# Edge matrix of a graph layer on one Trainium2 core: bank opening by one flag, matmuls in three rounds, 120 key columns

## The reference

```python
h = layernorm(x); acc = h
for _ in range(3):
    h = segment_sum(edge_weight[:, None] * h[dst], src)     # rows of h gathered and summed by node
    h = h / max(norm(h), 1e-12)
    acc = acc + h
x = x + acc / 4
x = x + layernorm(y + moe(y)) * gamma + beta                # y = layernorm(x)
```

## Time and profile before

| | us |
|---|---|
| median of 3 runs (1508.99 to 1516.28) | 1509.21 |
| the profiled execution | 1510.28 |
| its span in the trace | 1508.6 |
| TensorE matmuls busy | 1294.8 |
| DVE busy | 1113.5 |
| ACT busy | 883.1 |
| POOL busy | 248.7 |

### The profile page before, as it was taken

One profiled execution on the slowest core, in us unless ns is written; L12 is line 12 of the kernel. 1 busy time (PEld: TensorE's weight loads), 2 busy tenths in 40 slices (PEclk: granted clock), 3 DMA queues, 4 the chain that ended last, 5 costly groups with the idle time before them and its releaser, 6 DMA issues. The chain is left out here.

```text
span 1508.6 us, 31442 instructions
## 1 busy us (share of the span) xinstructions
PE 1294.8 (86%) x9378; PEld 1110.7 (74%) x9379; DVE 1113.5 (74%) x1946; ACT 883.1 (59%) x1937; POOL 248.7 (16%) x233
## 2 busy tenths in 40 slices
PE   4588888888799999999999999999977799999800
PEld 1466666767588888888888888888853799999800
DVE  8888989999676656766655766655567688998768
ACT  1678888888755555655555655555341566666522
POOL 1400000000040000000000000000031578887600
PEclk8799999999999999999999999999986899999955
DMA  5088888888886666656666656666322787334384
GB/s 186 28 207 196 201 199 197 203 202 209 216 233 208 184 184 180 194 170 189 182 189 184 190 164 185 178 189 182 113 91 89 238 272 218 108 105 106 89 289 143
DMA packets 225441, 267.36 MB, mean 177 GB/s; under 512 B 15763, under 2 KB 168066, under 8 KB 225298
## 3 DMA queue, kind: packets, MB, share of 16 engines
q1 hardware_dynamic: 211932, 240.41, 58.0%
q0 software_dynamic: 7680, 20.98, 4.8%
q10 hardware_dynamic: 5760, 5.25, 1.4%
HBM read 175.51 MB, written 91.07 MB: 177 GB/s over the span
## 5 line engine op out<-in xcount | busy, mean ns | idle before, releaser
L844 PE MATMUL ps_rows<-h_both,a_high 128*128 (+1 forms) x1875 | 506.2, 398 | 10.5 <-ACT halves L592 5.3
L684 DVE TENSOR_TENSOR a_low<-a_raw,a_high 128x640 fp32r<-128x640 f32 x375 | 305.6, 823 | 233.7 <-ACT a_high L578 230.4
L578 ACT ACTIVATE a_high<-a_raw 128x640 fp32r<-128x640 f32 x375 | 274.6, 740 | 287.6 <-PE ps_rows L847 265.6
L844 PEld LDWEIGHTS ps_rows<-h_both,a_high 128*128 128x128 f32 x1875 | 330.2, 191 | 68.6 <-ACT halves L592 14.4
L847 PEld LDWEIGHTS ps_rows<-h_both,a_low 128*128 128x128 f32 x1875 | 276.1, 191 | 32.9
L847 PE MATMUL ps_rows<-h_both,a_low 128*128 (+1 forms) x1875 | 284.9, 283 | 0.0
L821 PEld LDWEIGHTS ps_w<-lo_hot,key_w 128*128 128x128 bf16 x2736 | 196.1, 98 | 85.2 <-issue 83.9
L821 PE MATMUL ps_w<-lo_hot,key_w 128*128 128x160 bf16 x2736 | 211.4, 234 | 48.1 <-issue 38.0
L560 ACT ACTIVATE win<-ps_w 128x480 f32<-128x480 f32 x304 | 148.8, 575 | 56.3 <-PE ps_w L826 32.6
L668 DVE TENSOR_TENSOR key_w<-key_hot,tab_marks 128x1536 bf16<-128x1536 bf16 (+1 forms) x228 | 173.8, 817 | 0.0
L551 ACT ACTIVATE key_w<-key_hot,third_b 128x128 bf16<-128x128 bf16 x456 | 144.8, 428 | 5.6 <-DVE key_hot L659 3.1
(11 more groups left out here) (233 smaller groups left out, 1627.4 us busy)
## 6 DMA issues: line engine op xcount, KB each, us to landing
a_raw<-a_rows SPq DMA_DIRECT2D x375, 320.0 KB, 3.2
a_rows<-win SPq DMA_DIRECT2D x228, 240.0 KB, 3.6
w_raw<-in_L_ffn_w SPq DMA_DIRECT2D x32, 512.0 KB
a_rows<-win SPq DMA_DIRECT2D x76, 180.0 KB
b_t<-in_L_ffn_b ACTq DMA_DIRECT2D x40, 128.0 KB, 3.4
hf<-in_x SPq DMA_DIRECT2D x1, 3072.0 KB
x<-in_x SPq DMA_DIRECT2D x1, 3072.0 KB
tokens<-hf SPq DMA_DIRECT2D x4, 768.0 KB
```

The source lines that it names most:

```text
L578: a.activation(a_high[:, u, :], a_raw[:, u, :], ACT.Copy).then_inc(high_split, 1)
L684: v.tensor_tensor(a_low[:, u, :], a_raw[:, u, :], a_high[:, u, :].bitcast(F32), ALU.subtract).then_inc(low_split, 1)
L844: nc.tensor.matmul(ps[:, banks[w][r], :], a_high[:, u, r * P:(r + 1) * P], both, start=first, stop=False, skip_group_check=True)
```

## The change

It does these things:

- From batch 2 on the four opening matmuls write 16 columns in place of 512. In the first two batches, one for each half of PSUM, they still write 512.
- Columns that no matmul of a batch touches now keep what was there before. Two things follow. The carry must not read a stale window: `fresh` marks batches whose first window isn't shared with the batch before, and their carry reads the zero slot. And a batch's store may write stale rows past its last window, which later stores overwrite, except past the end: so the zeros over those rows are written last (`pad`, after load 14 of the first pass) from the zero slot of `win`, and SP's load of chunk 24 and POOL's constants wait for it. The padding at the start, its memset and its wait go.
- The 36 matmuls of a batch run in three rounds, one for each weight part, over the twelve steps. Each round waits for its own part alone.
- The key one-hots, their weighted copies, the stationary side of the matmuls and the rows of PSUM that they write have 120 columns (`M`) in place of 128.

```diff
@@ phase_tables
-            g.iota(tab.key_tab[:, 0:M, :], pattern=[[1, M], [0, 2]], base=0, channel_multiplier=0, **kw)
-            g.memset(tab.key_tab[:, M:P, :], -2.0)
+            g.iota(tab.key_tab[:], pattern=[[1, M], [0, 2]], base=0, channel_multiplier=0, **kw)
...
+            link(v.memset(fresh[:, 0:1], 0.0))
+            link(v.tensor_tensor(fresh[:, 1:s.NB], base[:, 1:s.NB], by_batch[:, 0:s.NB - 1, B - 1], ALU.subtract))
+            link(v.scalar_tensor_tensor(moved[:], fresh[:], float(B), moved[:], ALU.mult, ALU.add))
@@ phase_layers, sync
-            first = s.W * CW
-            sp.wait_ge(tabs, 3)
-            sp.dma_start(a_dram.rearrange("i (c n) l -> (i c) (n l)", c=CW)[first:s.CH * P, :],
-                         zeros[0:s.CH * P - first, :]).then_inc(padded, 16)
...
-            sp.wait_ge(padded, 16)
+            def pad():
+                for done in stored:
+                    sp.wait_ge(done, 16 * NB)
+                sp.dma_start(a_dram[s.W:s.W + PADDING, :, :].rearrange("i p l -> p i l"),
+                             win[0:M, 0, B * LO:(B + 1) * LO].unsqueeze(1).broadcast_to(
+                                 [M, PADDING, LO])).then_inc(padded, 16)
...
+                if j == CH - 1:
+                    sp.wait_ge(padded, 16)
                 load(0, j)
                 if j in LAST:
                     store(LAST[j], LAST[j] % WINS)
+                if j == PAD_AT:
+                    pad()
@@ gpsimd
             g.memset(none[:], 0.0).then_inc(tabs, 1)
-            g.memset(zeros[:], 0.0).then_inc(tabs, 1)
...
-            for done in stored:
-                pool.wait_ge(done, 16 * NB)
+            pool.wait_ge(padded, 16)
@@ vector
-                v.tensor_tensor(key_w[:, u, k, 0:n, :, :], key_hot[:, u, 0:n, :, :], mark(b, 2 + k, P)[:, 0:n, :, :],
+                v.tensor_tensor(key_w[:, u, k, 0:n, :, :], key_hot[:, u, 0:n, :, :], mark(b, 2 + k, M)[:, 0:n, :, :],
@@ tensor
+                wide = 16 if late(b, 2) else 512
                 for bank in range(BANKS):
-                    mm(ps_w[:, u, bank * 512:(bank + 1) * 512], none[:, 0:P], none[:, :],
+                    mm(ps_w[:, u, bank * 512:bank * 512 + wide], none[:, 0:P], none[:, 0:wide],
                        start=True, stop=False, skip_group_check=True)
...
-                pe.wait_ge(hot_ready, (b + 1) * 4)
-                pe.wait_ge(third_ready, (b + 1) * BY_ACT)
-                for j in range(B):
-                    for k in range(3):
-                        ins = mm(ps_w[:, u, bass.DynSlice(places[j], LO)], key_w[:, u, k, j // 2, :, j % 2],
+                for k in range(3):
+                    pe.wait_ge(hot_ready, b * 4 + (2 + k))
+                    if k == 2:
+                        pe.wait_ge(third_ready, (b + 1) * BY_ACT)
+                    for j in range(B):
+                        ins = mm(ps_w[0:M, u, bass.DynSlice(places[j], LO)], key_w[:, u, k, j // 2, :, j % 2],
                                  lo_hot[:, u, j // 2, :, j % 2],
                                  start=False, stop=False, skip_group_check=True)
```

More of the change, by code:

```diff
@@ L128, in phase_tables @@
         moved = sb("moved", [1, s.NB])
+        fresh = sb("fresh", [1, s.NB])
         fields = sb("fields", [1, s.NB, 2 * s.ROW])
@@ L378, in phase_layers @@
         LAST = {6: NB - 2, 10: NB - 1}
+        PAD_AT = 14
+        PADDING = -(-(CH * P) // CW) - s.W
         a_raw = sb("a_raw", [P, RING, G * P])
@@ L407, in phase_layers @@
             lo_hot, key_hot, key_w = [early.enter_context(nc.sbuf_tensor(name, shape, BF16)) for name, shape in (
-                ("lo_hot", [P, 2, PAIRS, LO, 2]), ("key_hot", [P, 2, PAIRS, P, 2]), ("key_w", [P, 2, 3, PAIRS, P, 2]))]
+                ("lo_hot", [P, 2, PAIRS, LO, 2]), ("key_hot", [P, 2, PAIRS, M, 2]), ("key_w", [P, 2, 3, PAIRS, M, 2]))]
             ps_w = early.enter_context(nc.psum_tensor("ps_w", [P, 2, BANKS * 512], F32))
@@ L411, in phase_layers @@
         ps = ctx.enter_context(nc.psum_tensor("ps_rows", [P, NBANK, 2 * D], F32))
-        zeros = a_raw[:].rearrange("p u c -> p (u c)")
         block = ctx.enter_context(nc.Block())
@@ L509, in _ @@
             g.memset(none[:], 0.0).then_inc(tabs, 1)
-            g.memset(zeros[:], 0.0).then_inc(tabs, 1)
             g.memset(win[:, :, B * LO:(B + 1) * LO], 0.0).then_inc(tabs, 1)
             g.memset(ones[:], 1.0).then_inc(tabs, 1)
-            pool.wait_ge(tabs, 4)
+            pool.wait_ge(tabs, 3)
             g.affine_select(out=ident[:], in_=ones[:], pattern=[[1, P]], compare_op=ALU.is_equal,
@@ L658, in one_hots @@
                     dve.wait_ge(third_ready, (b - 1) * BY_ACT)
-                v.tensor_tensor(key_hot[:, u, :, :, :], tab.key_tab[:].unsqueeze(1).broadcast_to([P, PAIRS, P, 2]),
-                                mark(b, 0, P), ALU.is_equal).then_inc(key_ready, 1)
+                v.tensor_tensor(key_hot[:, u, :, :, :], tab.key_tab[:].unsqueeze(1).broadcast_to([P, PAIRS, M, 2]),
+                                mark(b, 0, M), ALU.is_equal).then_inc(key_ready, 1)
                 v.tensor_tensor(lo_hot[:, u, :, :, :], tab.lo_tab[:].unsqueeze(1).broadcast_to([P, PAIRS, LO, 2]),
@@ L794, in _ @@
             mm = nc.tensor.matmul
-            pe.wait_ge(tabs, 5)
+            pe.wait_ge(tabs, 4)
             def multiply(b, i):
@@ L825, in multiply @@
                     pe.wait_ge(windows_out, b)
-                    ins = mm(ps_w[:, u, bass.DynSlice(places[0], LO)], ident[:, :],
+                    ins = mm(ps_w[0:M, u, bass.DynSlice(places[0], LO)], ident[:, 0:M],
                              win[:, (i - 1) % WINS, bass.DynSlice(slot, LO)],
@@ L1696, in __init__ @@
         self.lo_tab = sb("lo_tab", [P, s.LO, 2], BF16)
-        self.key_tab = sb("key_tab", [P, P, 2], BF16)
+        self.key_tab = sb("key_tab", [P, s.M, 2], BF16)
         self.marks = sb("tab_marks", [P, 5, s.STEPS], BF16)
```

## The result

| | before | after |
|---|---|---|
| median, us | 1511.90 (4 runs, 1508.99 to 1516.28) | 1561.47 (4 runs, 1560.03 to 1566.89) |
| ratio to before, 95% interval | | 1.0334 [1.0303, 1.0365] |
| the profiled execution | 1510.28 | 1562.75 |
| its span | 1508.6 | 1560.9 |

The change makes the kernel 3.3% slower; the forecast was 1570. It rested on +60.8 us, and +52.5 was measured between the profiled executions. From the page of the kernel after: the busy times, the TensorE clock granted in each fortieth of the span and the DMA share.

The account below looks back on a forecast made before the run. TensorE's sequencer was taken to bound the edge-matrix stage: 74 batches at 5.54 us give +62.7, the end -1.9, so +60.8 on 1510.3, less 1.1 to the median, is 1570 us; range 1496 to 1604.

Parts of the forecast that it names:

- The bound: Edge-matrix stage: TensorE's own sequencer sets the batch cycle, 4.65 us on average; the other engines wait for TensorE.
- The twelve addresses in round one: Edge matmuls: all twelve addresses are computed in the first round, taking the sequencer 2.1 us, and reused in later rounds.
- Rival (d): Edge matmuls: addresses are computed anew in each round, cycle 8.2 us, 1767 us in all; chance 0.06.
- The queue of 16 pairs: TensorE's queue: 14 of 30 weight-load and matmul pairs must start before the next load of places, 1.54 us.
- Rival (c): TensorE's queue is deeper and all 30 pairs fit, so no stall for room, cycle 4.7 us, 1505 us; chance 0.10.
- 120-column weight loads: Edge matmuls: the narrower stationary tile loses the fast path, 110 ns a pair in place of 71.
- rival (a): Edge matmuls: weight loads of 120 columns stay at 71 ns, cycle L + 3.55 = 5.09 us, 1534 us; chance 0.15.
- L: TensorE's register load of a batch's places: forecast 1.45 us, ends 0.9 and 1.9, depending on the stores' DMA share.
- The cycle: Edge-matrix batch on TensorE's sequencer: L + 4.1 against L + 3.0 before, forecast 5.54 us.
- Start: Before the first batches: memset gone, against low clock and starved round; net 0, ends -2.8 and +2.5 us.
- padding: Zeros issued late on SP, about 5 us, covered by chunks loaded ahead; taken at 0, end +5 us.
- Rival (b): Edge-matrix stage: the stores set the pace, 4.6 us a batch, so the kernel gets faster, 1498 us; chance 0.14.

Follow-up runs that it names:

- r1: The changed kernel with the 36 matmuls step by step again instead of in rounds, all else kept; 1500.08 us, ratio 0.9934 to the kernel before.
- r4: The kernel before with the three rounds alone added (128 columns, 512-column openers, early padding kept); 1553.48 us, ratio 1.0278.
- h1: The changed kernel with the rounds run over six steps at a time instead of twelve; ratio 0.9897 to the kernel before.
- k1: The changed kernel with the next batch's places loaded ahead of the third round in three of four batches; 1509.19 us, ratio 0.9974.
- r3: The changed kernel with openers of 512 columns in every batch; 1561.16 us, ratio 1.0346 to the kernel before.
- r1b: The changed kernel in step order, r1 run again beside r6; 1500.19 us, ratio 0.9924 to the kernel before.
- r6: The kernel before with the late padding alone (step order, 128 columns, openers of 512); 1503.45 us, ratio 0.9949.
- p1: The changed kernel, full rounds, with one register load of 16 words for two batches; ratio 1.0343 to the kernel before.
- p2: The step-order kernel r1 with one register load of 16 words for two batches; ratio 1.0109 to the kernel before.
- r2: The changed kernel with 128 key columns again; 1561.6 us, ratio 1.0324 to the kernel before.
- r5: The changed kernel without rounds and with 128 key columns, so narrow openers and late padding only; ratio 0.9923 to the kernel before.

## Why the prediction was right, and where it was wrong

- **The bound.** Right. TensorE's sequencer set the cycle, and the rounds lengthened just that. r1 and r4 show that the rounds carry the loss, h1 and k1 that they do so through what stands in the queue ahead of the load.
- **The twelve addresses in round one.** Right: 12 + 6 register instructions in 2.2 us, none in the rounds after, 12 matmuls in 2.10 us. Rival (d) falls.
- **The queue of 16 pairs.** Right, seen again at 219.5 and in 38 of 47 loads. Rival (c) falls, and k1 and h1 undo its effect. The Trainium skill's page "TensorE: Matmul & The Clock Gate" (spec table) gives the engine queue 64 entries. The traces disagree: the sequencer got at most 16 pairs, 32 instructions, ahead when it came to the load.
- **120-column weight loads.** Wrong term. I took 110 ns a pair from the f32 rows. The weight load itself did get longer, 97 to 133 ns, neither the old value nor the 180 I forecast; but a pair still takes 71, and the load lies beside the matmul before it. The Trainium skill, same page, Weight-path perf modes, has the fast weight load on when the number of weights is 128 and the type is not FP32; the trace agrees, with 97 ns for 128 columns and 133 for 120. The mistake was to take the spacing from f32 pairs (L847). Their matmuls have 256 moving columns: 117/256 is 0.46 ns a column, and 71/160 is 0.44. Both spacings fit the moving side, and neither says what a slower weight load costs. With 71 the rest of the cycle is rival (a)'s 3.55, and 3.72 was measured at full clock (r3). Some 0.1 of the 0.17 between is the turn of the loop, which the sum left out because it was read from one batch inside the loop: in r3's trace, from the end of a load to the start of the next, the batches inside take 3.59 to 3.67 us on average and the one in four where the loop turns 3.99. The remainder is not accounted for.
- **L.** Wrong term, the other way. I let L fall with the DMA share, 1.45 at 0.73; it was 1.71, at 0.75, where it had been 1.63. Over the kernels there is no such line: 1.79 at 0.78 (r3), 1.71 at 0.75 (after), 1.53 at 0.88 (r1b), 1.39 at 0.88 (h1), 1.19 at 0.85 (k1). What matters may be when the load falls, not how busy the stage is on average. In the batch above it begins in the quiet end of a batch and runs into the burst of stores; by stretch:

```profile
219.54:221.76 2.22, 1.29 (x19) 1.15 (x16) 2.01 (x3) 1.90 (x6) 0.00 (x0) 1.00 0.90 179
216.30:219.50 3.20, 3.20 (x31) 2.61 (x30) 2.79 (x4) 2.88 (x8) 0.00 (x0) 1.00 0.28 62
```

  DMA share is 0.90 during the load and 0.28 in the 3.2 us before it. This is argued from one batch; no run moved the stores against the load, so it stays open.
- **The clock.** I didn't count on dips; 0.90 was granted. Worth 3.86 - 3.72 = 0.14 us a batch outside L, and nothing in the time of the whole (r3).
- **The cycle.** Forecast 5.54 = 4.1 + 1.45, measured 5.57 = 3.86 + 1.71. (The equation T = 4.7 + 4.8/T gives 5.56, 1.6 us more over the stage.) The two wrong terms, -0.24 and +0.26, cancel, so that the cycle came out this close is luck; that it rose by some 0.9 us is the mechanism. With the right 71 ns a pair and the forecast L, rival (a)'s 1534 would have been the forecast, and it is 27 us too low. Over all 74 batches the forecast is 5.8 us too long (410.0 against 404.2): the first batches and the last, outside 100 to 360 us, run faster than the mean.
- **Start, end, padding.** Start forecast 0, measured -2.3, inside its bounds. End -1.9, measured -2.3 in the whole part behind the stage, and the 1.92 us wait of the earlier trace rows is gone from the trace. Nothing of the padding's +5 shows in the part behind the stage, and in a kernel that isn't bound by the rounds its move is worth 0.5% (r6).
- **What would show it.** Openers 5.57 apart (5.3 to 5.8), the first twelve at 0.175, DVE and ACT idle 1.4 to 1.5 us a batch, SP waiting for ACT, DMA 0.75 (0.73): all as told. The others at 0.071 in place of 0.11 and weight loads of 133 ns in place of 180: not. Rival (b) never came into play after, but may do in r1 and h1: with a cycle of 4.57 to 4.65 and SP not waiting for ACT, the stage there goes at the stores' old pace of 4.6. That this is what keeps them from going lower is argued; no run made the stores faster.

## What to carry to other kernels

When one engine also computes addresses, put the instructions that need new addresses evenly between those that don't: a reorder that changes no work moved the time by 3 to 4%. Issue a blocking load of registers while work already queued still runs, and don't put it behind more work than the queue holds; k1 got 3.5% back by that alone, though the queued work covered only half of its load. Look at more than the median of a time: the paired loads fell into two groups, and medians of 1.93 and 2.90 stood for the same mean. When a price is taken from a neighbouring row, look at what its spacing was bound by: the f32 pairs said nothing about bf16 pairs of 160 columns.

## What the runs showed of the hardware

- A bf16 weight load of 128x120 takes 133 ns where one of 128x128 takes 97, and with matmuls of 160 columns a pair takes 71 ns with either (24 in 1.70 us after, 36 in 2.55 before).
- TensorE's sequencer got at most 16 pairs of weight load and matmul ahead: a register load behind 30 pairs began with 15 or 16 left in 38 of 47 batches (after), one behind 18 with 12 or 13 (h1).
- Twelve addresses cost the sequencer 18 register instructions and 2.1 to 2.2 us, so a matmul that needs a new one follows the last after 0.175 us in place of 0.071 (after).
- A register load of 16 words took either 1.9 us or 2.9 to 3.7, 2.62 on average (p1, p2); one of 8 words took 0.59 at least and 1.68 on average after.
- With openers of 16 columns TensorE's granted clock fell to 0.90 over 100 to 360 us in rounds (after, r2), to 0.95 with the load early (k1) and to 0.97 in step order (r1, r5), but stayed at 1.00 in halves (h1); with openers of 512 it is 0.99 to 1.00 in either order. The dip looked at closely goes to the half level, 1.2 GHz: in the kernel after, the stretch 214.20 to 216.20 us was granted 0.50 and 216.30 to 220.10 1.00.
